# Two-layer AdaLN transformer: row maxima of attention taken for two heads at once, and PSUM banks moved from the second pass to the first

## The reference

```python
att = einsum('bthd,bThd->bhtT', q, k) * scale    # layer 0: -inf above the diagonal
att = softmax(att, axis=-1)                       # over 512 keys
out = einsum('bhtT,bThd->bthd', att, v)
y = out @ Wo + bo
x = x + ga * y
```

## Time and profile before

| | |
|---|---|
| median of 3 runs | 2424.55 us |
| lowest, highest | 2423.39, 2437.38 us |
| the profiled execution's own time | 2432.8 us |
| its span, first to last instruction | 2430.8 us |
| PE, DVE, ACT busy over the span | 1873.0, 1448.5, 1157.3 us |
| mean granted TensorE clock | 0.844 of 2.4 GHz |

### The profile page before, as it was taken

How to read it: one execution, slowest core, us unless ns; L and a number is a source line. 1 busy time by engine, 2 the same in 40 slices (tenths; PEclk the granted TensorE clock), 3 DMA queues, 4 the chain that set the end, 5 groups by cost and what they waited for, 6 DMA issues and landing times. The chain is left out here.

```text
span 2430.8 us, 43279 instructions
## 1 busy us (share of the span) xinstructions
PE 1873.0 (77%) x12804; PEld 976.6 (40%) x12868; DVE 1448.5 (60%) x2514; ACT 1157.3 (48%) x2802; POOL 892.7 (37%) x999
## 2 busy tenths in 40 slices
PE   5528999884618455629999999557999999999996
PEld 3314444432516334422222222234555555555552
DVE  4426767751401233317888888126888888888882
ACT  1115656560003111104667667305777677677672
POOL 3223344341140332310111111116666677666670
PEclk9768889895559765657999989758999999999997
DMA  3432323322013223232333332130111111111110
GB/s 107 133 101 74 112 92 107 108 84 84 14 63 103 83 85 101 72 94 72 99 108 108 104 105 80 65 111 25 31 48 31 33 43 38 39 52 41 38 49 20
DMA packets 137868, 179.90 MB, mean 74 GB/s; under 512 B 14896, under 2 KB 82355, under 8 KB 137520
## 3 DMA queue, kind: packets, MB, share of 16 engines
q1 hardware_dynamic: 135728, 174.59, 23.3%
q0 software_dynamic: 2048, 4.16, 0.6%
HBM read 97.22 MB, written 66.06 MB: 67 GB/s over the span
## 5 line engine op out<-in xcount | busy, mean ns | idle before, releaser
L910 DVE TENSOR_REDUCE M_sb<-banks 128x1 f32<-128x512 f32 (+3 forms) x1024 | 539.8, 581 | 228.0 <-PE banks L727 124.8
L812 ACT ACTIVATE probs_sb<-banks 128x512 f32<-128x512 f32 (+3 forms) x1024 | 473.5, 520 | 254.9 <-PE banks L753 250.8
L724 PE MATMUL banks<-K_sb,Q_sb 72*128 72x512 bf16 (+3 forms) x1024 | 373.8, 371 | 107.8 <-DMA V_sb<-v_dram 71.5
L753 PE MATMUL banks<-Q_sb,K_sb 75*128 75x512 bf16 (+3 forms) x1024 | 358.6, 357 | 5.9 <-ACT probs_sb L812 3.9
L767 PE MATMUL banks<-probs_sb,V_sb 128*32 128x512 f32 (+3 forms) x2048 | 249.9, 556 | 11.8 <-ACT osum_sb L823 8.6
L724 PEld LDWEIGHTS banks<-K_sb,Q_sb 72*128 72x128 bf16 x1024 | 103.2, 101 | 385.2 <-DVE M_sb L910 225.2
L1773 ACT ACTIVATE l_p_sb<-banks,l_nb_sb,l_inv_sb 128x128 f32<-128x128 f32 x512 | 228.0, 465 | 12.7 <-DVE l_nb_sb L1945 12.5
L1851 POOL TENSOR_TENSOR l_inv_sb<-l_clip_sb,l_minus_half_sb 128x16 f32<-128x16 f32 x64 | 186.2, 2909 | 57.2 <-DVE l_clip_sb L1920 55.3
L1859 POOL TENSOR_TENSOR l_pn_sb<-l_p_sb,l_rs_sb 128x512 f32<-128x512 f32 x128 | 150.1, 1173 | 145.5 <-DVE l_rs_sb L1951 144.0
L1844 POOL TENSOR_TENSOR l_ts_sb<-l_t_sb 128x1024 f32<-128x1024 f32 x64 | 153.4, 2396 | 41.1 <-DVE l_t_sb L1899 24.0
L1579 PE MATMUL banks<-lw_sb,l_xs_sb 128*128 128x512 f32 x256 | 127.8, 623 | 26.4 <-DMA l_xs_sb<-hx 22.8
(11 more groups left out here) (205 smaller groups left out, 3575.1 us busy)
## 6 DMA issues: line engine op xcount, KB each, us to landing
Q_sb<-qk_dram SPq DMA_DIRECT2D x192, 96.0 KB
v_dram<-vpad_sb SPq DMA_DIRECT2D x16, 1024.0 KB, 8.5
V_sb<-v_dram SPq DMA_DIRECT2D x64, 256.0 KB
o_dram<-osum_sb SPq DMA_DIRECT2D x64, 256.0 KB, 5.3
l_vs_sb<-l_vt_sb SPq DMA_DIRECT2D x112, 128.0 KB, 2.3
qk_dram<-parts_sb SPq DMA_DIRECT2D x96, 128.0 KB
K_sb<-qk_dram SPq DMA_DIRECT2D x32, 288.0 KB
x_norm_sb<-x SPq DMA_DIRECT2D x24, 256.0 KB, 2.7
```

The source lines that it names most:

```text
L724: mm = pe.matmul(out[:, 0:width], g.Q[0:RK, slot, h, k * P:(k + 1) * P], g.K[0:RK, slot, hk(h), 0:width], start=True, stop=not causal)
L753: pe.matmul(SB[ring % 3][:, t0:N], g.K[0:RM, q, hk(h), k * P:(k + 1) * P], g.Q[0:RM, q, h, t0:N], start=True, stop=True).then_inc(s["b_sco ...
L812: act.activation(g.probs[:, k, h, t0:N], SB[ring % 3][:, t0:N], ACT.Exp, scale=scale)\
L910: dve.reduce_max(g.M[:, u % 2, k, h:h + 1], SA[ring % 3][:, 0:width], AX.X, negate=True)\
```

## The change

The first pass gets two pairs of banks (0 to 3) and the second pass banks 4 and 5. a_tile writes the four banks in a ring; one DVE instruction at every odd head reduces both banks of a pair, 128 partitions x 2 x width, to two maxima, and adds 2 to the semaphore. A tile of even h waits for the pair of four and three tiles back; one of odd h doesn't wait. A b_tile waits for the exp of two tiles back.

```diff
-    SA, SB, OB, MB = g.bank[0:3], g.bank[3:6], g.bank[6], g.bank[7]
+    SA, SB, OB, MB = g.pair[0:2], g.bank[4:6], g.bank[6], g.bank[7]
@@ a_tile
-                out = SA[ring % 3]
+                out = SA[ring // 2 % 2][:, ring % 2, :]
...
-                if ring >= 3:
+                if ring >= 4 and h % 2 == 0:
                     pe.wait_ge(s["a_max"], i * 64 + n - 2)
                 elif ring == 0 and (u or lo):
                     pe.wait_ge(s["a_max"], i * 64 + n)
@@ b_tile
-                if ring >= 3:
-                    pe.wait_ge(s["exp"], i * 64 + n - 2)
+                if ring >= 2:
+                    pe.wait_ge(s["exp"], i * 64 + n - 1)
...
-                pe.matmul(SB[ring % 3][:, t0:N], g.K[0:RM, q, hk(h), k * P:(k + 1) * P],
+                pe.matmul(SB[ring % 2][:, t0:N], g.K[0:RM, q, hk(h), k * P:(k + 1) * P],
@@ exp
-                act.activation(g.probs[:, k, h, t0:N], SB[ring % 3][:, t0:N], ACT.Exp, scale=scale)\
+                act.activation(g.probs[:, k, h, t0:N], SB[ring % 2][:, t0:N], ACT.Exp, scale=scale)\
@@ maxima
-                dve.wait_ge(s["a_scores"], i * 64 + n + 1)
-                dve.reduce_max(g.M[:, u % 2, k, h:h + 1], SA[ring % 3][:, 0:width], AX.X, negate=True)\
-                   .then_inc(s["a_max"], 1)
+                if h % 2:
+                    dve.wait_ge(s["a_scores"], i * 64 + n + 1)
+                    dve.tensor_reduce(g.M[:, u % 2, k, h - 1:h + 1], SA[ring // 2 % 2][:, :, 0:width], AX.X,
+                                      ALU.max, negate=True).then_inc(s["a_max"], 2)
```

## The result

Over eight runs each, the kernel after takes 2454.56 us (median; 2446.84 to 2457.75), the kernel before on the same chip 2432.74 (2423.39 to 2443.18). The ratio is 1.0084, with a 95% interval of 1.0056 to 1.0112: some 20 us slower (14 to 27). The forecast of 2433 us was counted from the 2424.55 of three runs; eight runs of the same kernel give 2432.74, so the forecast to set beside the 20 is its +8. The time lies inside 2400 to 2470 and the slowdown in the likeliest class (within 1%), but rival B's +29 is nearer to 20 than my +8, so the rows have to tell which of the two it was. The profiled execution took 2448.02 us, with a span of 2446.1 against 2430.8.

The account below looks back on a forecast made before the run. PE in its written order bounds the kernel, DVE only where it stops PE. Layer 1's +12 and layer 0's -4.5 give +8 us, rounded, on the median 2424.55: 2433 us, range 2400 to 2470.

Parts of the forecast that it names:

- rival B: Clock: the stop at q=1 or small idles in every row lower it as now; +29 us, 2454; chance 0.20.
- The bound: Both attention stages: PE in its written order sets the time; DVE matters only where it stops PE.
- the row of layer 1: Steady row: b2 and b3 wait for the exp two tiles back, +0.25 us a row, +0.73 in row 2.
- The copy of L823 stands behind exp1 and delays neither: Layer 1: this ACT copy adds nothing to the waits for exp0 and exp1; regular unit forecast at 13.38 us.
- DVE: Maxima of L910: 512 instructions replace 1024, 522 us against 539.8, 18 us less busy, costed at nothing by itself.
- Unit 1: Rows 0 and 1 of q=1: the stop behind the reciprocals, 3.5 us per batch, goes and the clock stays up.
- the 0.7 that I left in row 1 of layer 0: Layer 0, q=1: 0.7 us per batch still lost in row 1, since a unit is shorter there.
- Rival C: The stop at q=1 stays and the row costs come on top: +57 us, 2482; chance 0.10.
- Rival A: Bank waits cost nothing and q=1 is freed: -67 us, about 2358, or half, 2391; chance 0.12.
- the sum of layer 0: Layer 0 in all -4.5 us: first batch +2.5, six batches -7, the last batch's parts cancel.
- 1.1 at the start of unit 2, whose first a (ring 0) waits for all maxima: Layer 0: a wait of 1.1 us per batch left at the start of unit 2.
- Layer 1's sum: Layer 1 in all +12 us: six batches +4, first batch +4.2, last +3.8.

Follow-up runs that it names:

- e1: Kernel before with only the second pass's third bank taken away (three single banks and two); ratio to the kernel before 1.0167.
- e4: Kernel after with ACT's copy of the turned maxima (L818) one exp later, behind exp (2, 1); ratio to the kernel before 1.0016.
- e2: Kernel after with four single banks and single maxima in place of two pairs, second pass still two banks; ratio to the kernel before 1.0066.
- h2: Kernel after without the reciprocals of L917, division replaced by a product with the sums (softmax not computed); ratio to the kernel before 1.0048.
- e3: Kernel after, but the ring's first tile waits for the pair two pairs back, not for all maxima; ratio to the kernel before 1.0033.
- h3: Kernel after with one bank in the second pass in place of two, one run; measured 3128.78 us.
- h1: Kernel before without the reciprocals of L917, division replaced by a product with the sums (softmax not computed); ratio to the kernel before 0.9861.

## Why the prediction was right, and where it was off

**The bound, and the row of layer 1: right.** b2 at +1.30 and b3 at +1.79 are the chain 0.65 + 0.60 + 0.05, and with the second exp's 0.49, to the hundredth; +0.25 a row and +0.71 for row 2 (forecast +0.73). e1 shows that the bank does it, e4 that the copy does its part.

**"The copy of L823 stands behind exp1 and delays neither": true, and yet row 1 was mis-sized.** Row 1 of layer 1, timeline before and then after: the last b, the copy that frees the output bank, and the PV matmuls.

```profile
1307.92 0.38 PE L753 MATMUL banks<-Q_sb,K_sb 75*128 75x512 bf16 x1
1308.00 0.60 ACT L823 ACTIVATE osum_sb<-banks 128x512 f32<-128x512 f32 x1
...
1308.75 1.07 PE L767 MATMUL banks<-probs_sb,V_sb 128*32 128x512 f32 x8
```

```profile
1350.49 0.60 ACT L823 ACTIVATE osum_sb<-banks 128x512 f32<-128x512 f32 x1
...
1350.66 0.39 PE L753 MATMUL banks<-Q_sb,K_sb 75*128 75x512 bf16 x1
...
1351.24 1.07 PE L767 MATMUL banks<-probs_sb,V_sb 128*32 128x512 f32 x8
```

The PV matmuls start 0.75 behind the copy's start in both, though b3 comes 0.08 before it in the one and 0.17 behind it in the other. Row 1 was 3.36 and stays 3.36. A wait that ends later than the new one hides it. I had this for layer 0 and missed it in layer 1. The unit is 13.12, not 13.38, and the six batches of layer 1 cost +0.8, not +4.

**DVE: right that it is worth nothing, half of the size.** 37 us of busy time gone, where 18 was forecast from durations with overlap; either is under PE. By the Trainium skill, "VectorE: DVE Perf Modes", section "The TRN2 errata — SBUF-src ops pay a fixed extra latency per instruction", it was an estimated 64. e2 gives the answer in time: without the pair 1.0066, with it 1.0084.

**Unit 1: right**, in six of seven batches of either layer; the 0.7 that I left in row 1 of layer 0 isn't there (10.35 to 10.57 from unit 0 to unit 1, against 10.36 for a unit). Rival C falls with it: it is e1's case, at 1.0167. Rival A fell with the rows.

**The step that failed is the sum of layer 0**, forecast -4.5, measured +4.9 in the profiled execution. The rows were right: 10.36 for a unit against 10.33, from +0.52, -0.05, +0.45 and -0.08 for rows 0 to 3 (2.43, 3.04, 2.71 and 2.17, against 1.91, 3.09, 2.26 and 2.25), where I had +0.44, +0.14, +0.45 and -0.22. The -0.22 is real with four single banks (row 3 is 2.02 in e2), and the pair takes most of it back, by ending late. The 9.4 us between them are these: the first batch took +6.65 us, not +2.5; the six behind it -3.9, not -7; the run-in before the first, +1.4, wasn't in the sum; and the last took +0.8, not 0. What was mis-sized is "1.1 at the start of unit 2, whose first a (ring 0) waits for all maxima". The stop is 1.22 to 1.31, so 1.1 was near, but I priced it without the halved clock behind it, which the same text counted at unit 1, and in the first batch not at all: I tied it to the reciprocals, and h2 shows that it doesn't need them. The clock fell behind it in three of seven batches. In two of these the interval is 1.5 us longer than in the others; in the first it is 14.14, where h2 with the same wait of 1.31 and a clock of 1.00 takes 11.68. That is an estimate of 5 to 6 us for the clock. e3 takes the wait away and gives 12 us. That this is also the distance from +8 to +20 is chance: 6.6 of it (1.1 in six batches) were in the sum already.

**Layer 1's sum: right by two errors, so by luck.** +11.4 against +12: row 1 cost nothing, and the first batch cost +7.3, not +4.2.

**Rival B** has a part in the extra cost, at the stops and not in the rows. Its condition, that each batch loses as much by the clock as before, didn't come: the mean clock of both stages rose by 0.03. In the steady units of the kernel after the clock stayed at 1.00, with PE standing 0.20 and 0.05 in each row (0.97 over the stage of layer 1); behind the stop in layer 0 it fell in three of seven batches. With one bank (h3) and idles of 0.26 in every 1.3 us it was 0.50 most of the time. The Trainium skill's rule on a clock that swings while TensorE cycles through banks ("TensorE: Matmul & The Clock Gate", "A second HAM failure mode: psum-queue depth-cycling") thus agrees with layer 0 of h3, where it goes to and fro, and not with the two-bank rows; in layer 1 of h3 it stayed low for most of the time. What lies between isn't settled.

**Where the gain went.** Without the reciprocals the kernel before is 34 us faster (h1): unit 1's stop wasn't worth more than that, since the next one takes its place. Of the 34 some 5 aren't the stop's: h1 also lacks the four reciprocals at the end of each layer, and from the load of the sums to the last projection it takes 6.8 us in place of 9.4. The change adds 46 us to that (h2 over h1), and the kernel after pays some 8 for its reciprocals (1.0084 against 1.0048, intervals that overlap), of which the same 5 stand at the ends of the layers. That -34 + 46 + 8 makes 20 is no test: each number is a difference of two of the same four times. The fourth bank is worth some 25 us, the third bank of the second pass some 41.

## What to carry to other kernels

A bank moved from one consumer to another is priced by the turn of a bank on either side: here matmul to exp 0.42, exp 0.60, 0.05 back, in a row whose tiles are 0.44 apart, so that two banks are late by a quarter of a microsecond in each row, with nothing to see in the sums of busy time. Price each stop with the clock behind it, as something that may come or not: 1.3 us cost up to 3.6, and the same wait in other batches no more than itself. And fusing two instructions of an engine that isn't the bound gives nothing, while its later end can hold the next tile; the slack came from the bank and not from the fusion.

## What had not been expected of the hardware

The pair of 128x1024 takes 1.215 us; four single maxima in a row take 2.48 and two pairs 2.35 to 2.36. Back to back, fusing saves 0.12 to 0.13 us in a row; most of what a second instruction adds is hidden by overlap. The clock: PE busy 4.21 of 5 us at 0.50 (h3), beside 1.00 in steady units where PE stands 0.20 and 0.05 in each row of 3.1 us, and the same wait of 1.22 us followed by 0.66 in one batch and by 1.00 in the next. And a kernel without its stops isn't free of them: with the reciprocals gone, the next load was late by 2.23 us and the clock fell to 0.50 behind it.
